# Gathering the dense products of a two-layer attention kernel into fewer key tiles

## The chip, the cores and the metric

The kernel runs on one core of one Trainium2 chip. The metric is the device time of one execution in microseconds, the median of several runs. TensorE is called PE below, its weight loads PEld, VectorE DVE, ScalarE ACT, GpSimd POOL and SyncE SP.

## The reference

Four sequences of 512 tokens with 256 channels pass through two attention layers with 16 heads of 16 channels.

```python
# layer 0
xn  = x * rsqrt(mean(x * x) + 1e-6) * rms_w
ss  = cond @ w_cond                         # scale, shift: 256 each
xm  = xn * (1 + scale) + shift
q, k, v = split(xm @ w_qkv)                 # q and k are rotated (rope)
x = softmax(q k^T / 4) v @ w_out + x
# layer 1
xn = layer_norm(x, norm_w, norm_b)
q, k, v = xn @ q_w + q_b, xn @ k_w + k_b, xn @ v_w + v_b      # and a mask
y  = softmax(q k^T + mask) v
e  = silu(cond) @ emb_w + emb_b             # scale, shift
h  = layer_norm(y, sb_norm_w, sb_norm_b) * (1 + scale) + shift
x  = x + silu(h) @ out_w + out_b
```

## The kernel before, in words

**Groups and key tiles.** The work is cut into 32 groups of four heads: groups 0 to 15 are layer 0, four for each batch, and 16 to 31 are layer 1. Step s of the main loop handles group s, in four key tiles k = 0 to 3 of 128 keys. A key tile (s, k) is the list `KEY_TILE`: four score products (L564) with four shift products that subtract the row maxima (L576), four row-score products of group s + 2 whose maxima DVE takes (L585, L961, and L958 in layer 1), and the product of the preceding key tile's probabilities with the values (L602). ACT takes the exponentials (L787). The first L602 of a tile's values is a good marker of time: `values(s, k)` stands near the end of tile (s, k + 1).

**One order for all engines.** `order()` writes out one list of operations. PE, ACT and DVE each walk through that list, so each meets its work in that order and waits there, in place, for what it needs. PE runs nothing out of order: if one operation in the list must wait, all behind it wait.

**Pieces.** Everything that isn't attention is cut into pieces, which the table `PIECES` puts into key tiles: `turn` (transposes of normalised tokens, L633), `qk` (one of four 128-channel chunks of queries and keys, L648), `v` (one of two halves of the values, L659), `y` (one of two halves of the output projection, L676), `modulate` and `embed` (the two products with the condition: step 0 at L687, step 1 at L695). The pieces of a tile stand behind its second row-score product and ahead of the other two.

**The row maxima's way back to PE.** The last row-score product of group n stands at the end of tile (n - 2, 3). DVE takes its maximum; then `negate(n)` on POOL (L1238, L1241, L1243) makes the shift; then `turn_shift(n)` on PE (L610), in tile (n - 1, 1) just ahead of the values, turns it. `turn_shift` waits for `negate`.

**POOL's program** is written out by hand and runs in order. For batch b of layer 1 it normalises the tokens (`normalise`), divides layer 0's outputs of the next batch by their sums (`divide`, without which `y` can't begin), splits query and key chunks into high and low parts (`split`, or `rope` for layer 0) and sends them to HBM through its own DMA queue (L1489), adds the values' bias (`add_bias`, L1299 and L1302, once for each half) and has the `negate` calls in between. SP loads the parts back (`operands`) and carries the shifts and outputs.

Of the kernel before, what the change touches and what calls it, by code (L numbers as in the profile page):

```python
# [12 lines left out]
P = 128  # L13
# [57 lines left out]
def v(layer, b):  # L71
    return ("v", layer, b, 0), ("v", layer, b, 1)
# [14 lines left out]
def one(pair):  # L87
# [34 lines left out]
for _b in range(B):  # L122
    STATISTICS[6 + NG * _b, 1] = ("p1", _b, 0)
    STATISTICS[6 + NG * _b, 2] = ("p1", _b, 1)
for _b in range(B - 1):
    STATISTICS[20 + NG * _b, 3] = ("f1", _b, None)

# [207 lines left out]
def build(nc, x, condT, mask, tables, vecs, w_cond, w_qkv, w_out, w_qkv1, v_b, emb_w, out_w, out_b, out):  # L335
# [4 lines left out]
    with ExitStack() as ctx:  # L340
# [39 lines left out]
        m.conditions = sb("conditions", [P, COND])  # L380
        m.chosen = sb("chosen", [P, B])
        m.e = sb("e", [P, KC, B])
        m.mod0_scale = sb("mod0_scale", [P, CT, B])
        m.mod0_shift = sb("mod0_shift", [P, CT, B])
        m.mod1 = sb("mod1", [P, 2, CT, B])
# [72 lines left out]
        q.es_step = sem("es_step")  # L458
        q.chosen_step = sem("chosen_step")
        q.acc_zero = sem("acc_zero")  # L460
# [87 lines left out]
def tensor(nc, pe, m, q):  # L548
# [131 lines left out]
    def conditioning(piece, vector):  # L680


        kind, step = piece
        if step == 0:
            bank = a_free(A[piece])
            for k in range(KC):
                last = nc.tensor.matmul(bank[W32 * k:W32 * (k + 1), :], vector[:, k, :], m.wc[:, k, :],  # L687
                                        start=True, stop=True, tile_position=(0, W32 * k), skip_group_check=True)
            last.then_inc(q.a_made, 1)
        else:  # L690
            bank = d_free(D[piece])
            pe.wait_ge(q.chosen_step, B)
# [84 lines left out]
def scalar(act, m, q):  # L777
# [27 lines left out]
    def tokens(piece):  # L805
        _, kind, b, h = piece
        use = USES.index((kind, b))
        if piece == ("turn", "p0", 0, 1):
            return
        if use >= 2 and kind != "f1":  # L810
            await_read(act, q, use - 2)
        to = m.xT[use % 2][:, h, :]
        if kind == "f1":
            act.wait_ge(q.d_done, D[piece] + 1)
            if b:
                act.wait_ge(q.silu_made, CT * (b - 1) + h + 1)
            act.activation(m.tanh[h], m.halved[h], ACT.Tanh).then_inc(q.tanh_made, 1)
            return
        bank = made(A[piece])
        if kind == "p0":  # L820
            if b:
                act.wait_ge(q.d_done, D["modulate", 1] + 1)
            act.wait_ge(q.mod_made, CT)
            act.activation(to, bank, ACT.Identity, bias=m.mod0_shift[:, h, b:b + 1], scale=m.mod0_scale[:, h, b:b + 1])\
# [79 lines left out]
    for op, *at in order():  # L904
# [6 lines left out]
        if op == "piece":  # L911
# [25 lines left out]
def vector(dve, m, q):  # L937
# [58 lines left out]

    def statistics(kind, b, src, t0, tiles):
        for t in range(t0, t0 + tiles):
            stat(dve.bn_stats(m.stats[:, TPB * b + t, :], src(t)))
# [16 lines left out]

    def take_statistics(kind, b, j):
        if kind == "p1":
            dve.wait_ge(q.d_done, D["y", 0, b, j] + 1)
            statistics(kind, b, lambda t: m.X[:, TPB * b + t, :], 2 * j, 2)  # L1020
        else:
            dve.wait_ge(q.d_done, D["output", NG * (B + b) + NG - 1] + 1)
            statistics(kind, b, lambda t: m.O[b % 2][:, t, :], 0, TPB)
        if j != 0:
            aggregate(kind, b)

    def opening():
# [50 lines left out]
    def rope_end(i):  # L1078
        dve.wait_ge(q.high_made, i + 1)
        dve.tensor_tensor(m.parts[:, 1, i, :], m.roped[0][i % 2][:, :], m.parts[:, 0, i, :], ALU.subtract)\  # L1080
           .then_inc(q.part_dve, 1)

    def modulate():
        bank = made(D["modulate", 1])[:, 0:KC * B].rearrange("p (k b) -> p k b", b=B)
        dve.wait_ge(q.vecs_in, 16)
        dve.tensor_copy(m.mod0_shift[:, :, :], bank[:, CT:2 * CT, :]).then_inc(q.mod_made, 1)
        dve.tensor_scalar(m.mod0_scale[:, 0, :], bank[:, 0, :], 1.0, m.vecs[:, RMS_W:RMS_W + 1], ALU.add, ALU.mult)\
           .then_inc(q.mod_made, 1)
        dve.tensor_scalar(m.mod0_scale[:, 1, :], bank[:, 1, :], 1.0, m.vecs[:, RMS_W + 1:RMS_W + 2], ALU.add, ALU.mult)\
           .then_inc(q.d_done, 1)  # L1090
# [4 lines left out]
        dve.tensor_scalar(m.xT[0][:, 1, :], half_turned, m.mod0_scale[:, 1, 0:1], m.mod0_shift[:, 1, 0:1],  # L1095
                          ALU.mult, ALU.add).then_inc(q.d_done, 1)
# [12 lines left out]
    def embed():  # L1109
        bank = made(D["embed", 1])[:, 0:KC * B].rearrange("p (k b) -> p k b", b=B)  # L1110
        dve.scalar_tensor_tensor(m.e[:, :, :], bank, 0.5,
                                 m.vecs[:, EMB_B:EMB_B + KC].unsqueeze(2).broadcast_to([P, KC, B]),
                                 ALU.mult, ALU.add).then_inc(q.d_done, 1)

# [90 lines left out]
def gpsimd(pool, m, q):  # L1205
# [57 lines left out]

    def rope(b, i, *shifts, send=True):


# [9 lines left out]
        pool.wait_ge(q.rope_pool, 4 * n + 2)  # L1276
        pool.tensor_tensor(x[:, :], x[:, :], z[:, :], ALU.add if two else ALU.subtract).then_inc(q.rope_pool, 1)
        pool.wait_ge(q.rope_pool, 4 * n + 3)
        await_parts(pool, q, b - 1, i)
# [3 lines left out]
        for n in shifts:  # L1283
            negate(n)
        if send:
            send_parts(b, i)

# [28 lines left out]
    for op, *at in order():  # L1316
        if op == "statistics" and at[2] != 0:
            moments_order.append(tuple(at[:2]))
    rstd_order = [u for u in NORMAL if u[0] != "p0"]
# [7 lines left out]
    pool.tensor_copy(m.ident16[:, :], m.ident[:, :]).then_inc(q.ident_made, 1)  # L1327
    pool.wait_ge(q.ident_made, 4)
    pool.tensor_copy(m.chosen[:, :], m.ident[:, 0:B]).then_inc(q.chosen_step, 1)
    for k in range(1, KC):  # L1330
        pool.wait_ge(q.chosen_step, k)
        pool.tensor_tensor(m.chosen[:, :], m.chosen[:, :], m.ident[:, W32 * k:W32 * k + B], ALU.add)\
            .then_inc(q.chosen_step, 1)
    for t in m.shift:
# [4 lines left out]
    for n in range(B):  # L1339
# [46 lines left out]
    negate(6)  # L1386
    divide(0, 0)
    divide(0, 1)
    rope(3, 0, 7)
    rope(3, 1, send=False)  # L1390

    def modulation():
        pool.wait_ge(q.d_done, D["embed", 1] + 1)
        for h in range(CT):
            for n, at in enumerate((SBN_W, SBN_B)):
# [25 lines left out]
    normalise(0)  # L1421
    send_parts(3, 1)
    divide(1, 0)
# [8 lines left out]
    split(B, 3)  # L1432
    add_bias(0, 0)
    for b in range(1, LAST):
# [4 lines left out]
        add_output_bias(b)  # L1439
        add_bias(b - 1, 1)  # L1440
        negate(NG * b + 9)
# [3 lines left out]
        split(B + b, 3)  # L1445
        add_bias(b, 0)
        divide(b + 1, 1)
# [3 lines left out]
    normalise(LAST)  # L1451
    add_output_bias(LAST)
    add_bias(LAST - 1, 1)
    negate(NG * LAST + 9)
# [216 lines left out]
```

## Time and profile before

| | |
|---|---|
| time of three runs | 492.68, 493.06, 494.52 us; median 493.06 us |
| the profiled execution | 493.28 us, span of its instructions 491.5 us |
| PE busy | 479.5 us, 98% |
| DVE, ACT, POOL busy | 79%, 70%, 64% |
| granted TensorE clock | 1.00 over the whole span |

The profiled execution is 0.22 us above the median of the runs. Busy time of PE is the union of overlapping products, and the end of each is modelled. So the start-to-start distances of PE's markers say more than its busy share.

### The profile page before, as it was taken

The page shows a single profiled execution, that of the slowest core. Times are in us where ns is not written, and L with a number is a line of the kernel's source. Part 1 is how long each engine was busy: PE and PEld are TensorE (multiplying, and loading weights), DVE is VectorE, ACT ScalarE, POOL GpSimd, SP SyncE. Part 2 cuts the span into 40 slices and gives each one's busy share as a digit, 9 for nine tenths or more (in the row PEclk, how much of TensorE's full clock was granted, in tenths as well). Part 3 has the DMA queues.
Part 4 walks back from the last instruction along what each step waited for, and adds up shares of the span by engine and source line. Part 5 has one row for each costly group of instructions (what it writes and reads, how often), then busy time and mean ns, then how long its engine had stood idle before and what let it go on. Part 6 is the DMA issues. An engine that isn't in the chain of part 4 may idle for free.

```text
span 491.5 us, 9721 instructions
## 1 busy us (share of the span) xinstructions
PE 479.5 (98%) x3205; PEld 178.4 (36%) x3205; DVE 386.1 (79%) x990; ACT 342.7 (70%) x676; POOL 314.2 (64%) x447
## 2 busy tenths in 40 slices
PE   7999899999999999999999999999999999999996
PEld 3563322323333334333343234333333323333234
DVE  3767896998886688856887688967899999999224
ACT  1662467898767786867767776776787778777853
POOL 6569976888798898699737692739991055005501
PEclk9999999999999999999999999999999999999999
DMA  7775157444423365225412361104411121111011
GB/s 244 197 206 194 45 135 264 112 115 149 112 66 115 111 183 149 68 68 140 123 54 67 107 187 44 46 24 126 114 45 44 45 88 45 44 45 45 2 43 43
DMA packets 41577, 49.79 MB, mean 101 GB/s; under 512 B 12388, under 2 KB 34036, under 8 KB 41272
## 3 DMA queue, kind: packets, MB, share of 16 engines
q1 hardware_dynamic: 33336, 31.84, 22.6%
q0 software_dynamic: 7904, 16.03, 10.9%
q10 hardware_dynamic: 288, 1.31, 0.8%
q8 instruction: 25, 0.41, 0.4%
q14 instruction: 24, 0.20, 0.1%
HBM read 27.62 MB, written 19.01 MB: 95 GB/s over the span
## 4 chain that ended last, share of the span: by engine, by line
PE 79%; DVE 14%; issue 3%; POOL 2%; ACT 1%; DVEq 0%; POOLq 0%; ACTq 0%
PE bank L602 20%; PE bank L648 12%; PE bank L576 11%; PE bank L585 11%; PE bank L564 9%; DVE masked L958 8%; PE bank L659 6%; PE bank L676 5%; DVE row_max L961 2%; PE bank L633 2%; ACT probs L787 1%; PE bank L617 1%; PE bank L610 1%; PE bank L734 1%; POOL shift L1335 1%
## 5 line engine op out<-in xcount | busy, mean ns | idle before, releaser
L787 ACT ACTIVATE probs<-bank 128x512 f32<-128x512 f32 x512 | 270.2, 599 | 71.3 <-PE bank L576 70.6
L961 DVE TENSOR_REDUCE row_max<-bank 128x1 f32<-128x512 f32 x256 | 159.9, 681 | 38.1 <-PE bank L585 37.9
L585 PE MATMUL bank<-k_s,q_s 64*128 64x512 f16 x512 | 179.9, 382 | 2.1 <-DVE row_max L961 1.2
L958 DVE CUSTOM_DVE_ANT_0 masked<-bank,mask_bias 128x512 bf16<-128x512 f32 x256 | 162.1, 687 | 20.3 <-PE bank L585 19.6
L564 PE MATMUL bank<-q_s,k_s 64*128 64x512 f16 x512 | 151.3, 380 | 0.3
L576 PE MATMUL bank<-shift,kx 64*128 64x512 f16 x512 | 148.7, 376 | 0.0
L602 PE MATMUL bank<-probs,v_aug 128*17 128x512 f32 x1024 | 135.4, 598 | 0.7 <-ACT probs L787 0.7
L585 PEld LDWEIGHTS bank<-k_s,q_s 64*128 64x128 f16 x512 | 46.2, 93 | 154.6 <-DVE row_max L961 67.4
L1238 POOL TENSOR_SCALAR scaled<-row_max 128x16 f32<-128x16 f32 x30 | 7.7, 256 | 86.3 <-DVE row_max L958 49.0
L648 PE MATMUL bank<-xT,wqkv 128*128 128x512 f32 x128 | 59.6, 605 | 1.0 <-DVE xT L1095 0.6
L576 PEld LDWEIGHTS bank<-shift,kx 64*128 64x128 f16 x512 | 46.9, 95 | 33.4
L1489 POOL DMA_DIRECT2D q_parts<-parts x60 | 34.8, 585 | 5.7 <-ACT parts L895 4.8
L1489 POOL DMA_DIRECT2D k_parts<-parts x62 | 35.1, 572 | 3.4 <-ACT parts L895 3.3
L564 PEld LDWEIGHTS bank<-q_s,k_s 64*128 64x128 f16 x512 | 32.8, 94 | 11.7 <-ACT probs L787 7.4
L648 PEld LDWEIGHTS bank<-xT,wqkv 128*128 128x128 f32 x128 | 22.9, 189 | 30.0 <-issue 26.9
L659 PE MATMUL bank<-wqkv,xT 128*128 128x256 f32 x128 | 31.3, 389 | 0.0
L602 PEld LDWEIGHTS bank<-probs,v_aug 128*17 128x17 f32 x1024 | 17.8, 95 | 30.6 <-ACT probs L787 14.5
L676 PE MATMUL bank<-wo,xT 128*128 128x256 f32 x112 | 27.9, 392 | 0.0
L659 PEld LDWEIGHTS bank<-wqkv,xT 128*128 128x128 f32 x128 | 23.2, 190 | 8.6 <-issue 5.4
L1015 DVE TENSOR_TENSOR X<-bank,X 128x512 f32<-128x512 f32 x14 | 9.6, 687 | 18.7 <-PE bank L676 18.7
L849 ACT ACTIVATE plain<-bank 128x512 f32<-128x512 f32 x16 | 9.5, 595 | 19.7 <-PE bank L648 19.7
L676 PEld LDWEIGHTS bank<-wo,xT 128*128 128x128 f32 x112 | 20.1, 189 | 8.1 <-DVE row_max L958 3.0
(122 smaller groups left out, 480.6 us busy)
## 6 DMA issues: line engine op xcount, KB each, us to landing
q_s<-q_parts SPq DMA_DIRECT2D x32, 256.0 KB, 3.3
k_s<-k_parts SPq DMA_DIRECT2D x32, 256.0 KB, 4.4
k_parts<-parts POOLq DMA_DIRECT2D x62, 128.0 KB, 3.2
q_parts<-parts POOLq DMA_DIRECT2D x60, 128.0 KB, 3.0
X<-in_x SPq DMA_DIRECT2D x4, 512.0 KB, 7.1
O<-oT SPq DMA_DIRECT2D x64, 32.0 KB, 2.0
roped<-inverses SPq DMA_DIRECT2D x16, 128.0 KB
y<-X SPq DMA_DIRECT2D x7, 256.0 KB, 2.2
```

The costliest lines, as they stand in the source:

```text
L564: nc.tensor.matmul(bank, m.k_s[slot][rows, i, keys], m.q_s[slot][rows, i, :], start=True, stop=False)
L576: nc.tensor.matmul(a_bank(m, A["score", s, k, h]), keys, m.shift[s % SHIFTS][rows, i, :], start=False, stop=True).then_inc(q.a_made, 1)
L585: nc.tensor.matmul(bank, m.q_s[slot][rows, i, queries], m.k_s[slot][rows, i, :], start=True, stop=True).then_inc(q.d_made, 1)
L602: last = nc.tensor.matmul(m.ACC[W32 * h:W32 * h + W, :], m.v_aug[pu % VALUES][:, k, G * g + h, :], m.probs[k][:, h, :], start=(k == 0), st ...
L633: last = nc.tensor.transpose(bank[:, t * P:(t + 1) * P], src[:, t, h * P:(h + 1) * P], m.ident[:, :])
L648: last = nc.tensor.matmul(bank, m.wqkv[layer][:, k, i * P:(i + 1) * P], m.xT[use % 2][:, k, :], start=(k == 0), stop=(k == CT - 1))
L659: last = nc.tensor.matmul(bank[:, t * C:(t + 1) * C], m.xT[use % 2][:, k, at], m.wqkv[layer][:, k, 2 * C:3 * C], start=(k == 0), stop=(k = ...
L676: last = nc.tensor.matmul(bank[:, t * C:(t + 1) * C], m.xT[use % 2][:, k, at], m.wo[layer][:, k, :], start=(k == 0), stop=(k == CT - 1))
L787: act.activation(m.probs[k][:, h, :], bank, ACT.Exp, scale=1.0 if s >= B * NG else float(DH) ** -0.5)\
L958: dve.tensor_tensor_reduce(m.masked[D["max", n, k, h] % ND][:, :], bank, m.mask_bias[:, b, :], 1.0, LOWEST, ALU.add, ALU.max, to)\
L961: dve.tensor_reduce(to, bank, AX.X, ALU.max).then_inc(q.d_done, 1)
L1489: engine.dma_start(to, m.parts[:, part, i, :]).then_inc(signal, 16)
```

## The change

The pieces are laid together. For every batch both halves of `y` of layer 0 stand in tile (6 + 4b, 1), where one stood in tile 0 and one in tile 1; both halves of the values stand in tile (6 + 4b, 2), where the first half stood earlier, in a tile of its own ((4, 2) for batch 3 of layer 0, (9 + 4b, 0) for layer 1); all four query and key chunks of a layer-1 batch stand in tile (7 + 4b, 3), where chunks 2 and 3 stood in tile (8 + 4b, 1). The last batch's values stand together in tile (20, 3). The statistics of a batch's four token tiles are all taken in tile (6 + 4b, 2).

The condition's product is turned by four transposes with the identity, where eight instructions multiplied it with a matrix `chosen` that POOL built; DVE adds the four partial rows with a reduction. One token tile of the opening's normalisation goes from DVE to ACT. Two small operations on `e` go from DVE to POOL.

On POOL, `rotate(3, 0)` stands between the two divisions of batch 0, the parts of `rope(3, 1)` are sent at once, and both halves of `add_bias(b - 1)` stand behind all splits of batch b, ahead of `divide(b + 1, 1)`. Before, one half of `add_bias(b - 1)` stood ahead of `negate(4b + 9)` and one half of `add_bias(b)` stood at the later place.

```diff
-    4: ((), (), v(0, 3)[:1], ()),
...
-    _other = v(0, 3)[1:] if _b == 0 else v(1, _b - 1)[1:]
-    PIECES[_s] = (*one(y(0, _b)), _other, ())
-    PIECES[_s + 1] = ((), (), turn("p1", _b), qk(1, _b, 0, 1))
-    PIECES[_s + 2] = ((), qk(1, _b, 2, 3), (), ())
-    PIECES[_s + 3] = (v(1, _b)[:1], (), (), ())
-PIECES[20] = ((), qk(1, LAST, 2, 3), (), v(1, LAST)[:1])
-PIECES[21] = (v(1, LAST)[1:], (), (), ())
+    PIECES[_s] = ((), y(0, _b), v(1, _b - 1) if _b else v(0, 3), ())
+    PIECES[_s + 1] = ((), (), turn("p1", _b), qk(1, _b, 0, 1, 2, 3))
+PIECES[20] = ((), (), (), v(1, LAST))
...
-    STATISTICS[6 + NG * _b, 1] = ("p1", _b, 0)
-    STATISTICS[6 + NG * _b, 2] = ("p1", _b, 1)
+    STATISTICS[6 + NG * _b, 2] = ("p1", _b)
...
-                last = nc.tensor.matmul(bank[:, c * B:(c + 1) * B], m.conditions[:, c * P:(c + 1) * P], m.chosen[:, :],
-                                        start=True, stop=True)
+                last = nc.tensor.transpose(bank[:, c * P:(c + 1) * P], m.conditions[:, c * P:(c + 1) * P], m.ident[:, :])
...
+            if piece == ("modulate", 0):
+                act.wait_ge(q.rstd0_made, 1)
+                act.activation(m.XN[0][:, TPB - 1, :], m.X[:, TPB - 1, :], ACT.Copy,
+                               scale=m.rstd["p0"][:, TPB - 1:TPB]).then_inc(q.xn0_made, 1)
...
-        for t in range(TPB):
+
+        for t in range(TPB - 1):
             normal_tile(dve, m, "p0", m.X[:, 0:TPB, :], m.XN[0], t, t).then_inc(q.xn0_made, 1)
...
+        dve.tensor_reduce(m.mod0[:, :, :], by_chunk(made(D["modulate", 1])), AX.X, ALU.add).then_inc(q.mod_made, 1)
...
     divide(0, 0)
+    rotate(3, 0)
     divide(0, 1)
-    rope(3, 0, 7)
-    rope(3, 1, send=False)
+    rotated_parts(3, 0, 7)
+    rope(3, 1)
...
     normalise(0)
-    send_parts(3, 1)
     divide(1, 0)
...
     split(B, 3)
-    add_bias(0, 0)
     for b in range(1, LAST):
         normalise(b)
         divide(b + 1, 0)
         if b == 1:
             add_output_bias(0)
         add_output_bias(b)
-        add_bias(b - 1, 1)
         negate(NG * b + 9)
         for i in range(3):
             split(B + b, i)
         negate(NG * b + 10)
         split(B + b, 3)
-        add_bias(b, 0)
+        add_bias(b - 1, 0)
+        add_bias(b - 1, 1)
         divide(b + 1, 1)
         negate(NG * b + 11)
         if b == 1:
             modulation()
     normalise(LAST)
     add_output_bias(LAST)
+    add_bias(LAST - 1, 0)
     add_bias(LAST - 1, 1)
     negate(NG * LAST + 9)
```

## Rows read from the trace of the kernel before

**Rows 1.** The page: span, and busy time of PE.

```profile
span 491.5 us, 9721 instructions
...
PE 479.5 (98%) x3205; PEld 178.4 (36%) x3205; DVE 386.1 (79%) x990; ACT 342.7 (70%) x676; POOL 314.2 (64%) x447
```

**Rows 2.** The chain that ended last: start, length, engine, output, line, instructions.

```profile
10.78 0.88 DVE XN L932 x3
11.80 1.08 PE bank L633 x8
...
25.30 6.87 PE bank L648 x16
...
94.80 0.99 PE bank L695 x8
...
128.30 0.98 PE bank L602 x8
130.04 1.92 PE bank L676 x8
...
154.73 3.63 PE bank L648 x8
```

**Rows 3.** Timeline of PE, values of tiles (6, 2) and (6, 3): start, length.

```profile
143.99 1.05 PE L602 MATMUL bank<-probs,v_aug 128*17 128x512 f32 x8
...
146.48 1.05 PE L602 MATMUL bank<-probs,v_aug 128*17 128x512 f32 x8
```

**Rows 4.** Timeline of PE, the values behind `turn_shift` of groups 8, 10, 14, 18, 22.

```profile
149.41 1.05 PE L602 MATMUL bank<-probs,v_aug 128*17 128x512 f32 x8
...
179.51 1.05 PE L602 MATMUL bank<-probs,v_aug 128*17 128x512 f32 x7
...
235.35 1.08 PE L602 MATMUL bank<-probs,v_aug 128*17 128x512 f32 x8
...
291.30 1.08 PE L602 MATMUL bank<-probs,v_aug 128*17 128x512 f32 x8
...
351.22 1.08 PE L602 MATMUL bank<-probs,v_aug 128*17 128x512 f32 x8
```

**Rows 5.** Timeline of POOL: `negate` 8, 9, 10, 13, 14, `add_bias`, `divide`, `negate` 17, 18, 21, 22.

```profile
148.30 0.27 POOL L1238 TENSOR_SCALAR scaled<-row_max 128x16 f32<-128x16 f32 x1
...
161.24 0.25 POOL L1238 TENSOR_SCALAR scaled<-row_max 128x16 f32<-128x16 f32 x1 [2.95 <-DVE row_max L961]
...
176.25 0.25 POOL L1238 TENSOR_SCALAR scaled<-row_max 128x16 f32<-128x16 f32 x1
...
217.07 0.25 POOL L1238 TENSOR_SCALAR scaled<-row_max 128x16 f32<-128x16 f32 x1 [0.50 <-DVE row_max L961]
...
230.67 0.25 POOL L1238 TENSOR_SCALAR scaled<-row_max 128x16 f32<-128x16 f32 x1 [0.20 <-DVE row_max L961]
...
235.70 0.93 POOL L1299 TENSOR_SCALAR v_bias<-vb_row,vecs 128x256 f32<-128x256 f32 x1
...
239.24 1.27 POOL L1312 TENSOR_TENSOR xT<-O,roped 128x512 f32<-128x512 f32 x1
...
272.99 0.25 POOL L1238 TENSOR_SCALAR scaled<-row_max 128x16 f32<-128x16 f32 x1 [3.31 <-DVE row_max L958]
...
287.32 0.25 POOL L1238 TENSOR_SCALAR scaled<-row_max 128x16 f32<-128x16 f32 x1
...
330.37 0.25 POOL L1238 TENSOR_SCALAR scaled<-row_max 128x16 f32<-128x16 f32 x1 [7.57 <-DVE row_max L958]
...
348.06 0.25 POOL L1238 TENSOR_SCALAR scaled<-row_max 128x16 f32<-128x16 f32 x1
```

**Rows 6.** Timeline of DVE: the statistics of a half batch.

```profile
195.97 0.74 DVE L999 BATCH_NORM_STATS2 stats<-X 128x6 f32<-128x256 f32 x2
```

**Rows 7.** Timeline of PE in the opening; in brackets the idle time before.

```profile
1.17 5.37 PE L702 MATMUL bank<-idle 128*128 128x512 f16 x17 [1.17 <-DVE idle L1028]
8.56 1.06 PE L687 MATMUL bank<-wc,condT 128*32 128x512 f32 x8 [2.01 <-DMA wc<-in_w_cond]
```

More of the change, by code:

```diff
@@ L458, in build @@
         q.es_step = sem("es_step")
-        q.chosen_step = sem("chosen_step")
+        q.embed_step = sem("embed_step")
         q.acc_zero = sem("acc_zero")
@@ L823, in tokens @@
             act.wait_ge(q.mod_made, CT)
-            act.activation(to, bank, ACT.Identity, bias=m.mod0_shift[:, h, b:b + 1], scale=m.mod0_scale[:, h, b:b + 1])\
+            act.activation(to, bank, ACT.Identity, bias=m.mod0[:, CT + h, b:b + 1], scale=m.mod0_scale[:, h, b:b + 1])\
                 .then_inc(q.a_done, 1)
@@ L995, in write_output, with statistics @@
            .then_inc(q.d_done, 1)
-    def statistics(kind, b, src, t0, tiles):
-        for t in range(t0, t0 + tiles):
+    def statistics(kind, b, src):
+        for t in range(TPB):
             stat(dve.bn_stats(m.stats[:, TPB * b + t, :], src(t)))
@@ L1015, in residual, with take_statistics @@
         dve.tensor_tensor(to, bank.rearrange("p (t c) -> p t c", c=C), to, ALU.add).then_inc(q.d_done, 1)
-    def take_statistics(kind, b, j):
+    def take_statistics(kind, b):
         if kind == "p1":
-            dve.wait_ge(q.d_done, D["y", 0, b, j] + 1)
-            statistics(kind, b, lambda t: m.X[:, TPB * b + t, :], 2 * j, 2)
+            dve.wait_ge(q.d_done, D["y", 0, b, 1] + 1)
+            statistics(kind, b, lambda t: m.X[:, TPB * b + t, :])
         else:
             dve.wait_ge(q.d_done, D["output", NG * (B + b) + NG - 1] + 1)
-            statistics(kind, b, lambda t: m.O[b % 2][:, t, :], 0, TPB)
-        if j != 0:
-            aggregate(kind, b)
+            statistics(kind, b, lambda t: m.O[b % 2][:, t, :])
+        aggregate(kind, b)
     def opening():
@@ L1081, in rope_end, with by_chunk @@
            .then_inc(q.part_dve, 1)
+    def by_chunk(bank):
+        return bank.rearrange("p (c k w) -> p c w k", k=KC, w=W32)[:, :, 0:B, :]
     def modulate():
[L1084 removed]
+        dve.tensor_reduce(m.mod0[:, :, :], by_chunk(made(D["modulate", 1])), AX.X, ALU.add).then_inc(q.mod_made, 1)
         dve.wait_ge(q.vecs_in, 16)
[L1086 to L1087 removed]
+        dve.wait_ge(q.mod_made, 1)
+        dve.tensor_scalar(m.mod0_scale[:, 0, :], m.mod0[:, 0, :], 1.0, m.vecs[:, RMS_W:RMS_W + 1], ALU.add, ALU.mult)\
            .then_inc(q.mod_made, 1)
[L1089 to L1090 removed]
+        dve.tensor_scalar(m.mod0_scale[:, 1, :], m.mod0[:, 1, :], 1.0, m.vecs[:, RMS_W + 1:RMS_W + 2],
+                          ALU.add, ALU.mult).then_inc(q.d_done, 1)
         half_turned = made(D["turn", "p0", 0, 1])
@@ L1109, in embed @@
     def embed():
[L1110 to L1113, printed above, removed]
+        dve.tensor_reduce(m.e[:, :, :], by_chunk(made(D["embed", 1])), AX.X, ALU.add).then_inc(q.d_done, 1)
     def last_batch():
@@ L1262, in split, with rotate @@
         send_parts(pu, i)
-    def rope(b, i, *shifts, send=True):
+    def rotate(b, i):
         side, two = divmod(i, 2)
@@ L1277, in rope, with rotated_parts @@
         pool.tensor_tensor(x[:, :], x[:, :], z[:, :], ALU.add if two else ALU.subtract).then_inc(q.rope_pool, 1)
+    def rotated_parts(b, i, *shifts):
+        n = 4 * (b - 1) + i
+        x = m.roped[0][0]
         pool.wait_ge(q.rope_pool, 4 * n + 3)
@@ L1284, in rope @@
             negate(n)
-        if send:
-            send_parts(b, i)
+        send_parts(b, i)
+    def rope(b, i, *shifts):
+        rotate(b, i)
+        rotated_parts(b, i, *shifts)
     def add_bias(b, j):
@@ L1316, in gpsimd @@
     for op, *at in order():
-        if op == "statistics" and at[2] != 0:
-            moments_order.append(tuple(at[:2]))
+        if op == "statistics":
+            moments_order.append(tuple(at))
     rstd_order = [u for u in NORMAL if u[0] != "p0"]
@@ L1327, in gpsimd @@
     pool.tensor_copy(m.ident16[:, :], m.ident[:, :]).then_inc(q.ident_made, 1)
[L1328 to L1333, printed above, removed]
     for t in m.shift:
@@ L1349, in gpsimd @@
             pool.wait_ge(q.xn0_made, TPB)
+            pool.wait_ge(q.d_done, D["modulate", 1] + 1)
             for a in range(2):
@@ L1387, in gpsimd @@
     divide(0, 0)
+    rotate(3, 0)
     divide(0, 1)
-    rope(3, 0, 7)
-    rope(3, 1, send=False)
+    rotated_parts(3, 0, 7)
+    rope(3, 1)
     def modulation():
         pool.wait_ge(q.d_done, D["embed", 1] + 1)
+        pool.tensor_scalar(m.e[:, :, :], m.e[:, :, :], 0.5, None, ALU.mult).then_inc(q.embed_step, 1)
+        pool.wait_ge(q.embed_step, 1)
+        pool.tensor_tensor(m.e[:, :, :], m.e[:, :, :],
+                           m.vecs[:, EMB_B:EMB_B + KC].unsqueeze(2).broadcast_to([P, KC, B]), ALU.add)\
+            .then_inc(q.embed_step, 1)
+        pool.wait_ge(q.embed_step, 2)
         for h in range(CT):
```

9 lines of the change are left out of this document (4 added, 5 removed).

## The prediction

> **What bounds the kernel now.** I read the page first. PE is busy for 98% of the span [rows 1], so one may think that only less PE work can help. Next I read the chain of waits. From step 6 to step 20 it is PE's own lines one after another, and the timeline of PE shows the same as a rhythm: two plain key tiles lie 146.48 - 143.99 = 2.49 us apart [rows 3], and a tile with pieces is longer by the pieces' own time. So PE sets the pace, and the other three engines follow with some slack. How much slack is what decides here. PE meets its waits in order, so a result that comes late stops everything behind it. The timeline of POOL shows where the slack is small. In the first row of [rows 5] `negate(8)` begins at 148.30, and the values that stand behind its turn begin at 149.41 [rows 4]: 1.11 us from the start of `negate` to that marker when PE is already there and waits. The marker before it is at 146.48 [rows 3], so that tile took 2.93 us against 2.49: PE lost some 0.45 us there, to POOL. Everywhere else PE comes later than POOL. I take 1.11 us as the price from `negate` to the marker, and ask for each later `negate` how long ahead of PE it was, and how much PE work the change removes between its two ends.
>
> **What the change saves on PE.** A block of eight fp32 instructions (one half of `y` or of the values) takes 1.92 us in the chain, a block of twice the work 3.63 us [rows 2]. Two blocks laid together therefore save 2 x 1.92 - 3.63 = 0.21 us, the cost of going from the half-height fp16 products to full fp32 ones and back. Sixteen instructions took 6.87 us in the opening, where other fp32 work follows [rows 2]; with one way back of some 0.2 us that is 7.05, and 2 x 3.63 - 7.05 = 0.21 us again. Blocks that vanish: four of `y`, four of `qk`, four of `v` in the tiles (6 + 4b, 2), one for the last batch: 13 x 0.21 = 2.7 us. The bounds are 13 x 0.15 and 13 x 0.3, 2 to 4 us.
>
> The embed step of 0.99 us becomes four transposes; eight take 1.08 us [rows 2], so 0.54, a saving of 0.45 us at most, 0.35 taken. In the opening the chain goes over DVE's normalisation, 0.88 us for three tiles [rows 2]; a fourth moved to ACT takes 0.29 us off it. ACT has just copied the condition and is idle. Since a later DMA wait may swallow some of this, I take 0.2 us, bounds 0 and 0.3. The turned condition of the opening is made while DVE still normalises, so its shorter form is hidden behind that. The extra reduction and its wait on DVE (three small operations before, three after) come to nothing within 0.1 us; the transposes of the tokens run meanwhile. The two operations on `e` fall on POOL behind `negate(15)`, where it next waits for statistics. If that cover were gone they would cost some 0.5 us.
>
> The statistics of the first two token tiles, 0.74 us [rows 6], move one tile down, into DVE's queue ahead of the maxima of tile (6 + 4b, 2). PE is then in the 3.63 us block of the values and DVE would be idle. Without this cover they would delay the maxima by 0.74 us for each batch, 3 us in all; I take nothing.
>
> Batch 0's `negate(8)` gets away from its wait: the `y` block is one tile later but the parts of `rope(3, 1)` are sent ahead of it, and `normalise(0)` begins when the statistics do, 4 to 5 us behind the `y` block's tile. By the same sum as above it ends about 1.5 us before PE comes. That gives back the 0.45 us. Savings together: 2.7 + 0.35 + 0.2 + 0.45 = 3.7 us.
>
> **What it costs: the `negate` behind the splits.** All four chunks now stand in tile (7 + 4b, 3), ahead of the last row scores of group 9 + 4b. POOL waits for that group's maxima in `negate(9 + 4b)` (the releaser in the brackets is DVE's row_max [rows 5]), then does a rope or three splits with their sends, then `negate(10 + 4b)`. That POOL work is as long as before. But between the same two ends PE had chunks 2 and 3, 3.63 us, and a first half of the values, 1.92 us, together 5.55 us, and both are gone from there: six plain tiles remain, 6 x 2.49 = 14.9 us. The slack before was:
>
> - Batch 0: `negate(10)` begins at 176.25, plus 1.11 is 177.36; the marker is at 179.51 [rows 4, 5]. Slack 2.15, so PE waits 5.55 - 2.15 = 3.4 us. From the other side: POOL's work from 161.24 to 176.25 is 15.0 us without a gap.
> - Batch 1: 230.67 + 1.11 against 235.35, slack 3.57, and POOL's own wait of 0.20 goes too. PE waits 5.55 - 3.77 = 1.8 us.
> - Batch 2: 287.32 + 1.11 against 291.30, slack 2.87: 2.7 us. The same POOL work took 14.33 us here and 13.60 for batch 1, 0.2 of it a wait; without that stretch it would be 1.8 us. I take 2.3.
> - Batch 3: from `negate(21)` to `negate(22)` lie four splits; 348.06 + 1.11 against 351.22, slack 2.05. Here 3.63 goes, and of the values 2 x 1.92 become 3.63, which still stand in this stretch. PE waits 3.63 + 0.21 - 2.05 = 1.8 us.
>
> Sum: 3.4 + 1.8 + 2.3 + 1.8 = 9.3 us.
>
> **What it costs: `add_bias` ahead of `divide`.** For batches 1 and 2 POOL then has `negate`, one split, now four token tiles of bias in place of two, and `divide(b + 1, 1)`, for which `y` waits. Two token tiles take 239.24 - 235.70 = 3.54 us [rows 5]. From the start of `negate(14)` to the end of the division: 235.70 - 230.67 = 5.03, plus 2 x 3.54, plus 1.27, together 13.4 us. PE, which has just been released, has 1.11 us to its marker, three plain tiles of 2.49, and 130.04 - 128.30 = 1.74 us [rows 2] from that marker to the `y` block: 10.3 us. So it waits 3.1 us more in batch 1. In batch 2, a layer-1 tile with a turned output lies between, some 0.6 us by the row of the transposes: 2.5 us more. Both waits stop PE with scores, maxima and exponentials queued behind them. Nothing makes up for it, since PE sets the pace after them too. For batch 0 the division stands right behind one split and is early. Sum: 5.6 us. The bounds of both sums: if POOL gained 1 us in each of the four stretches, 9.3 + 5.6 would be 10.9; if the stretch of batch 2 repeats and transfers stretch others alike, some 17.
>
> SP is passed too: `operands(12)` waits for the parts of `rope(3, 3)`, which POOL now sends later by the wait in `negate(9)`. Row scores of group 12 begin two steps on, and I count at least 3 us of slack, so nothing; if it is gone, the same 2 to 3 us of delay would show as a wait for `k_s`.
>
> **The sum.** 493.3 - 3.7 + 9.3 + 5.6 = 504.5 us for a profiled execution, 504.3 against the median.
>
> **The rivals.**
>
> *PE alone counts (faster).* If POOL is ahead of each `turn_shift` and each `y`, only the savings are left: 493.1 - 3.7 = 489.4 us. For it speaks that PE shows hardly a wait now. It needs POOL to save over 3.4 us of its 15 us between `negate(9)` and `negate(10)`, and nothing in the diff takes an operation out of there. It decides from that point: as long as the slack lost is above the slack of 2 to 3.8 us shown, PE stops. Chance 0.07.
>
> *The `negate` waits come, the `y` waits don't.* If `add_bias` runs in gaps, 489.4 + 9.3 = 498.7 us. Against it: POOL has no gap between `negate(14)` and the division. Chance 0.08.
>
> *The clock falls.* PE would stand still for 3.4, 3.1, 2.5 us at three places. The longest stop in the trace that didn't lower the clock is 2.01 us [rows 7]: the granted clock is 1.00 throughout. What a low clock costs shows in the opening: 17 idle products took 5.37 us where full speed (2.4 GHz, 0.213 us each, the step of 1.2 GHz being 0.43) takes 3.6, so 1.75 us. Three such places: 5 us more, 509.5. Chance 0.12. The Trainium skill, TensorE: Matmul & The Clock Gate, Part 1, says that a gate halves PE's clock after idling and opens it again after activity; by it this rival is what a stop of this kind does, and no row here has a stop so long.
>
> *Little change.* Savings and waits cancel if only one of the six waits comes and is small: within 0.5% (some 2.5 us, which is about what a measurement here can tell from no change). Chance 0.04.
>
> **How the numbers follow.** The forecast of 504.3 us has 0.69. The bounds of its terms, savings of 3 to 5 us and waits of 11 to 17, give 499 to 507. With the clock rival above it and the second rival below, the range 498.5 to 509 us leaves out the faster and the small cases and the tails. Faster 0.07, same 0.04, slower 0.89.
>
> **What would show it.** In the profile after, the tile behind `turn_shift(10)` has a gap on PE of about 3.4 us, with the releaser L1243 on POOL; so have groups 14, 18 and 22 with 1.8 to 2.7. The `y` products of tiles (14, 1) and (18, 1) wait for L1312. Tiles with two halves are 2.49 + 3.63 us apart and the tile with four chunks 9.5. POOL shows no idle time from `negate(13)` to `divide(2, 1)`. If these gaps are missing or POOL is idle there, the prediction is wrong. It is wrong too if the row scores or DVE are what PE waits for after the 7 us block, or if a granted clock below 1 shows behind a gap.

## The result and the profile after

The changed kernel takes 508.99 us (507.76 to 511.14, 4 runs) against 492.87 us (492.66 to 494.52, 4 runs): a ratio of 1.033, interval 1.029 to 1.036. The forecast was 504.3 us, with a range of 498.5 to 509.0. The profiled execution took 509.28 us, its span is 507.1 us, 15.6 us more than before [rows 1].

The page of the changed kernel, span and busy time:

```profile
span 507.1 us, 9703 instructions
...
PE 481.4 (95%) x3197; PEld 182.3 (36%) x3197; DVE 385.5 (76%) x989; ACT 343.0 (68%) x677; POOL 313.7 (62%) x445
```

PE has about as much work as before (479.5 us) and 15.6 us more span. The view of waits says for whom PE waited: line and releaser, us in total, times, longest.

```profile
PE bank L603 <- POOL neg_max L1240: 9.0, 4, 3.3
PE bank L669 <- POOL xT L1317: 4.6, 2, 3.4
PE bank L680 <- DMA wc<-in_w_cond: 1.3, 1, 1.3
...
PE bank L569 <- DMA shift<-shift_rows: 0.7, 1, 0.7
```

The timeline of PE has each of these waits; the number in brackets is the idle time ahead of the instruction.

```profile
128.16 0.39 PE L569 MATMUL bank<-shift,kx 64*128 64x512 f16 x2 [0.70 <-DMA shift<-shift_rows]
...
180.97 0.22 PE L603 MATMUL bank<-ident,neg_max 128*32 128x128 f16 x1 [3.31 <-POOL neg_max L1240]
...
238.04 0.22 PE L603 MATMUL bank<-ident,neg_max 128*32 128x128 f16 x1 [1.68 <-POOL neg_max L1240]
...
250.81 5.38 PE L669 MATMUL bank<-wo,xT 128*128 128x256 f32 x16 [3.40 <-POOL xT L1317]
...
301.16 0.22 PE L603 MATMUL bank<-ident,neg_max 128*32 128x128 f16 x1 [2.42 <-POOL neg_max L1240]
...
313.94 3.69 PE L669 MATMUL bank<-wo,xT 128*128 128x256 f32 x16 [1.23 <-POOL xT L1317]
...
366.78 0.22 PE L603 MATMUL bank<-ident,neg_max 128*32 128x128 f16 x1 [1.60 <-POOL neg_max L1240]
```

L603 is `turn_shift` of groups 10, 14, 18 and 22, L669 `y` of batches 2 and 3. The timeline of POOL answers to [rows 5]: `negate` 9 and 10, then 13 and 14, the first `add_bias`, and the division.

```profile
164.89 0.25 POOL L1235 TENSOR_SCALAR scaled<-row_max 128x16 f32<-128x16 f32 x1 [7.12 <-DVE row_max L957]
...
180.00 0.25 POOL L1235 TENSOR_SCALAR scaled<-row_max 128x16 f32<-128x16 f32 x1
...
223.58 0.25 POOL L1235 TENSOR_SCALAR scaled<-row_max 128x16 f32<-128x16 f32 x1 [8.37 <-DVE row_max L957]
...
237.07 0.25 POOL L1235 TENSOR_SCALAR scaled<-row_max 128x16 f32<-128x16 f32 x1
...
242.11 0.93 POOL L1304 TENSOR_SCALAR v_bias<-vb_row,vecs 128x256 f32<-128x256 f32 x1
...
249.41 1.26 POOL L1317 TENSOR_TENSOR xT<-O,roped 128x512 f32<-128x512 f32 x1
```

From `negate(9)` to `negate(10)` POOL takes 15.1 us, before 15.0; from 13 to 14 it takes 13.5, from 14 to the end of the division 13.6 where the prediction had 13.4. POOL's work is what it was, and from `negate(13)` to the end of the division it stands idle for 0.2 us only. What changed is that PE has less to do meanwhile. And POOL now stands idle for 7 to 8 us ahead of `negate(9)` and `negate(13)`, behind which its longest stretches begin.

One line above is odd. The `y` block of 16 instructions takes 5.38 us at 250.81 and 3.69 us at 313.94. The view by windows shows why; the columns are the stretch, its length, busy time and count for PE, PEld, DVE, ACT and POOL, the granted clock, the DMA share and GB/s.

```profile
246.00:252.00 6.00, 2.60 (x18) 1.23 (x11) 2.32 (x8) 2.32 (x5) 5.32 (x9) 0.94 0.38 112
252.00:258.00 6.00, 6.00 (x31) 3.60 (x31) 2.46 (x5) 1.22 (x3) 2.06 (x9) 0.78 0.00 0
...
300.00:305.00 5.00, 3.84 (x22) 1.37 (x23) 1.79 (x8) 1.35 (x3) 4.69 (x10) 0.74 0.74 225
305.00:312.00 7.00, 7.00 (x56) 1.84 (x54) 6.38 (x20) 5.10 (x10) 6.22 (x9) 0.94 0.33 99
```

The granted clock falls to its lower level, 1.2 GHz, for some 3 us behind two of the waits. It stays at 1.00 behind the other waits, behind the first one of 3.31 us too (windows 180 to 184 and 184 to 188). The four runs have mean clocks of 0.993, 0.989, 0.993 and 0.989: in each of them it fell somewhere.

**The balance,** by the distances of the values' markers against those of before: the four waits for `negate` cost 3.50, 1.87, 2.62 and 1.79 us, together 9.8; the two waits for the division 3.4 and 1.3, together 4.7; the low clock 1.75 us in the first `y` block and 1.54 us in tile (17, 2), which took 4.66 in place of 3.12 us; the late shift of group 6 in tile (6, 0) 1.48 us (0.70 of it is the wait for L569, the rest is spread over the tile). That is 19.2 us of loss for 15.6 us of span, so 3.6 us were saved. Added up from the tiles themselves, the savings are 3.7 us: 2.6 us for the thirteen blocks (0.20 each), 0.40 for the embed tile (3.07 in place of 3.47 us), 0.45 for tile (7, 1), and 0.25 in the opening.

### The profile page after: what moved, and what is told of

Same layout as the page of the kernel before. It is cut to its first block, busy times and chain, and to the rows that moved or that the text cites. A ratio compares the mean times of both kernels' runs of the same rounds, so it can differ in the third digit from the quotient of the medians.

```text
span 507.1 us, 9703 instructions
## 1 busy us (share of the span) xinstructions
PE 481.4 (95%) x3197; PEld 182.3 (36%) x3197; DVE 385.5 (76%) x989; ACT 343.0 (68%) x677; POOL 313.7 (62%) x445
## 4 chain that ended last, share of the span: by engine, by line
PE 49%; POOL 19%; DVE 16%; issue 6%; DMA 4%; ACT 1%; SPq 0%; DVEq 0%; POOLq 0%; ACTq 0%
PE bank L595 13%; DVE masked L954 9%; PE bank L569 7%; PE bank L641 6%; PE bank L578 6%; PE bank L557 6%; PE bank L669 5%; POOL k_parts L1495 3%; PE bank L652 3%; DMA k_parts<-parts 3%; POOL q_parts L1495 3%; POOL parts L1257 2%; DMA sums<-oT 2%; POOL roped L1273 2%; POOL roped L1270 1%
## 5 line engine op out<-in xcount | busy, mean ns | idle before, releaser
L569 PE MATMUL bank<-shift,kx 64*128 64x512 f16 x512 | 149.5, 378 | 0.7 <-DMA shift<-shift_rows 0.7
L569 PEld LDWEIGHTS bank<-shift,kx 64*128 64x128 f16 x512 | 46.9, 95 | 34.9 <-DMA shift<-shift_rows 1.2
L641 PE MATMUL bank<-xT,wqkv 128*128 128x512 f32 x128 | 58.5, 602 | 1.0 <-DVE xT L1095 0.6
L669 PE MATMUL bank<-wo,xT 128*128 128x256 f32 x112 | 28.5, 406 | 4.6 <-POOL xT L1317 4.6
L652 PE MATMUL bank<-wqkv,xT 128*128 128x256 f32 x128 | 30.0, 385 | 0.0
L595 PEld LDWEIGHTS bank<-probs,v_aug 128*17 128x17 f32 x1024 | 17.8, 95 | 29.3 <-ACT probs L779 16.1
L669 PEld LDWEIGHTS bank<-wo,xT 128*128 128x128 f32 x112 | 21.6, 200 | 11.8 <-issue 4.7
```

What stands on the lines that cost most here:

```text
L569: nc.tensor.matmul(a_bank(m, A["score", s, k, h]), keys, m.shift[s % SHIFTS][rows, i, :], start=False, stop=True).then_inc(q.a_made, 1)
L595: last = nc.tensor.matmul(m.ACC[W32 * h:W32 * h + W, :], m.v_aug[pu % VALUES][:, k, G * g + h, :], m.probs[k][:, h, :], start=(k == 0), st ...
L641: last = nc.tensor.matmul(bank, m.wqkv[layer][:, k, i * P:(i + 1) * P], m.xT[use % 2][:, k, :], start=(k == 0), stop=(k == CT - 1))
L652: last = nc.tensor.matmul(bank[:, t * C:(t + 1) * C], m.xT[use % 2][:, k, at], m.wqkv[layer][:, k, 2 * C:3 * C], start=(k == 0), stop=(k = ...
L669: last = nc.tensor.matmul(bank[:, t * C:(t + 1) * C], m.xT[use % 2][:, k, at], m.wo[layer][:, k, :], start=(k == 0), stop=(k == CT - 1))
```

## The experiments

Every kernel is timed together with the kernel before on the same chip; ratios are to it. Times in the expectations are medians, waits are those of profiles. The changed kernel is the base of each edit, unless the text says otherwise.

### Keeping PE busy in its waits

PE runs products of zeros, which belong to nothing, into the bank that is free anyway, ahead of each long wait and for less time than it.

```diff
+        keep_busy({10: 14, 14: 6, 18: 9, 22: 6}.get(n, 0), bank)      # in turn_shift
...
+                keep_busy({2: 14, 3: 5}.get(b, 0), bank)              # in tokens_out, layer 0
```

> The changed kernel with 54 idle products of PE in all, each batch of them just ahead of a wait of PE and shorter than that wait: 14, 6, 9 and 6 ahead of turn_shift 10, 14, 18 and 22, and 14 and 5 ahead of y of batches 2 and 3. They add nothing to the reference's result. Theory (the granted clock falls because PE stood still): the clock is 1.00 everywhere, the y block of batch 2 takes 3.6 us in place of 5.4, tile (17, 1) 3.1 in place of 4.7, the waits end at the same times, and the time falls by 3.3 us, to about 505.6 us. Rival (these stretches are slow for another reason, such as memory contention with POOL): no gain, 508.9 us or up to 1 us more.

506.52 us (506.38 to 506.81), ratio 1.027, interval 1.025 to 1.029. All four runs have a mean clock of 1.00, and they lie within 0.43 us, where those of the changed kernel lie within 3.4 us. The `y` block of batch 2 in PE's timeline, and the windows around it:

```profile
249.62 3.69 PE L673 MATMUL bank<-wo,xT 128*128 128x256 f32 x16 [0.43 <-POOL xT L1321]
```

```profile
240.00:250.00 10.00, 9.56 (x66) 3.30 (x63) 6.97 (x18) 6.15 (x13) 9.06 (x13) 1.00 0.54 144
250.00:260.00 10.00, 10.00 (x59) 6.33 (x57) 5.76 (x19) 3.63 (x9) 3.90 (x14) 1.00 0.06 13
```

The block takes 3.69 us again. (The slow tile that the expectation calls (17, 1) is (17, 2), by the distances of the markers; it takes 3.10 us here.) So the 5.38 us were the clock's, and the clock fell because PE stood still; POOL and the DMA queues had the same work in both. The gain in the medians is 2.5 us, less than the 3.3 us that one profile showed. Part of it came back as waits, since POOL's results are no earlier: tile (18, 1) took 9.12 us in place of 7.42, with five idle products and then 1.73 us of waiting for the division of batch 3, where PE waited 1.23 us in all. Part of the gain isn't the clock's either: between the two profiles 0.74 us lie in tile (6, 0) and 0.30 us in tile (2, 0), which vary from profile to profile.

### The bias ahead of `negate`

```diff
+        add_bias(b - 1, 0)
+        add_bias(b - 1, 1)
         negate(NG * b + 9)
...
-        add_bias(b - 1, 0)
-        add_bias(b - 1, 1)
         divide(b + 1, 1)
```

> The changed kernel with both halves of add_bias(b - 1) ahead of negate(4b + 9) in place of ahead of divide(b + 1, 1). POOL had 8.4 and 10.5 us without work there. Theory (POOL's program between negate(14) and the division is what y waits for): the two waits of PE for L1317, 3.40 and 1.23 us, vanish, the clock doesn't fall behind the first one (1.75 us back), and the four waits for negate stay as they are: 508.9 - 4.7 - 1.75, about 502.5 us. Rival (POOL is short of time as a whole, so its work only moves): negate(13) and negate(17) come late instead, and the time stays within 1.5 us of 508.9.

504.38 us (499.87 to 504.66), ratio 1.020, interval 1.016 to 1.025. The view of waits has no L1317 any more, and the four waits for `negate` stand at 9.2 us in all. So `add_bias` was what made `y` wait, and POOL had room for it elsewhere. The time is 1.9 us above the theory's, and its four runs say why: three with a mean clock of 0.99 took 504.3 to 504.7 us, the one with 1.00 took 499.87. In the profiled run the clock fell behind the first wait, of 3.35 us, which in the changed kernel's profile had left it alone (tile (9, 2) took 3.77 us for 2.49), and again in tile (17, 2), 4.66 us. The run at 1.00 is 4.4 to 4.8 us faster than the others, more than the 3.0 us that tiles (9, 2), (9, 3) and (17, 2) lost in the profile; where the rest went isn't known, since only one run has a trace.

### The chunks two and two

```diff
-    PIECES[_s + 1] = ((), (), turn("p1", _b), qk(1, _b, 0, 1, 2, 3))
-PIECES[20] = ((), (), (), v(1, LAST))
+    PIECES[_s + 1] = ((), (), turn("p1", _b), qk(1, _b, 0, 1))
+    PIECES[_s + 2] = ((), qk(1, _b, 2, 3), (), ())
+PIECES[20] = ((), qk(1, LAST, 2, 3), (), v(1, LAST))
```

> The changed kernel with chunks 2 and 3 back in tile (8 + 4b, 1); y and the values stay gathered. Theory (the gathered chunks take 3.63 us of PE work out of the stretch between two negates): the four waits for negate vanish, since only 1.9 us or less are missing there against a slack of 2.05 or more; y of batches 2 and 3 still waits, but only some 1.3 us each; the clock stays at 1.00. Four blocks more cost 4 x 0.21 us. 508.9 - 9.8 - 2.1 - 3.3 + 0.8, about 494.5 us. Rival (the gathered values cost most of it): above 500 us.

495.10 us (494.61 to 496.24), ratio 1.004, interval 1.003 to 1.006, clock 1.00 in all runs. One edit of a table brings back 13.9 of 16.1 us. The view of waits has no line for `negate`; the two waits for the division are left:

```profile
243.11 3.69 PE L670 MATMUL bank<-wo,xT 128*128 128x256 f32 x16 [1.59 <-POOL xT L1318]
...
301.17 3.69 PE L670 MATMUL bank<-wo,xT 128*128 128x256 f32 x16 [1.78 <-POOL xT L1318]
```

The gathered values, 1.9 us taken out of the same stretch, were within the slack of 2.05 us and more. Gathering the chunks wasn't.

### `negate` one split earlier

```diff
     rope(3, 3)
-    split(B, 0)
     negate(10)
+    split(B, 0)
...
-        for i in range(3):
+        for i in range(2):
             split(B + b, i)
         negate(NG * b + 10)
```

`negate(11)` and `negate(22)` move likewise, and part of the last batch's work behind `negate(22)` changes places.

> The changed kernel with each negate behind the splits moved ahead of one more split (negate(11) and negate(22) too), and nothing else: POOL does the same work up to each division. Theory (in batches 1 and 2 it is POOL's whole work up to divide that sets the end, not the place of negate): the waits for negate vanish, 9.8 us, but y of batches 2 and 3 now waits about 5 and 4 us in place of 3.4 and 1.2, so that only the parts of batch 0 and batch 3 and some of the clock come back: 508.9 - 3.5 - 1.8, about 503.5 us, with the clock falling behind one or both waits for y. Rival (the waits are separate from each other): all 9.8 us and one fall of the clock come back, about 497.5 us.

509.22 us (507.18 to 509.98), ratio 1.032, interval 1.029 to 1.034. The theory's two waits are there, and so are things that it didn't have:

```profile
183.96 0.39 PE L569 MATMUL bank<-shift,kx 64*128 64x512 f16 x2 [1.17 <-DMA shift<-shift_rows]
...
250.50 5.38 PE L669 MATMUL bank<-wo,xT 128*128 128x256 f32 x16 [3.96 <-POOL xT L1317]
...
313.67 6.43 PE L669 MATMUL bank<-wo,xT 128*128 128x256 f32 x16 [5.41 <-POOL xT L1317]
```

The waits for `negate` are gone and the waits for `y` have grown from 4.6 to 9.4 us: up to the division POOL has the same work, and PE is at the same place whichever of the two it waits for. That part stands. But the time is 5.7 us above what I expected. Both `y` blocks now run at the low clock (5.38 and 6.43 us). Shifts come late through SP's queue, and tiles (10, 0), (10, 1) and (14, 0) take 4.74, 7.74 and 4.46 us, 5.8 us more than in the changed kernel; two of the experiments below look into that.

### Half of the values back in tile (4, 2)

```diff
+    4: ((), (), v(0, 3)[:1], ()),
```

> The changed kernel with the first half of the values of batch 3 of layer 0 back in tile (4, 2). Theory (the wait for the shift of group 6 in tile (6, 0), 1.5 us, comes since PE is 1.9 us nearer to POOL's parts of batch 2, and SP's queue holds the shift behind the loads that wait for those parts): the wait vanishes, one more block costs 0.2 us, and the time is about 1.3 us lower, 507.6 us, which the times may hardly show but the profile does. Rival (rotate(3, 0) or the other order on POOL holds SP back): the wait stays and the time is 0.2 us higher.

509.00 us (507.32 to 510.54), ratio 1.032, interval 1.030 to 1.034. The wait for L569 is gone from the profile. SP's queue shows where it had come from. First the changed kernel, then this one: the last load of an inverse, the queries and keys of group 8, and the shift of group 6.

```profile
117.89 0.61 SPq L1574 DMA_DIRECT2D roped<-inverses  x1
123.84 0.36 SPq L1525 DMA_DIRECT2D q_s<-q_parts  x1
124.26 0.46 SPq L1525 DMA_DIRECT2D k_s<-k_parts  x1
124.82 0.61 SPq L1550 DMA_DIRECT2D sums<-oT  x1
125.53 1.38 SPq L1542 DMA_DIRECT2D shift<-shift_rows  x2
```

```profile
120.32 0.62 SPq L1575 DMA_DIRECT2D roped<-inverses  x1
121.12 0.36 SPq L1526 DMA_DIRECT2D q_s<-q_parts  x1
...
123.78 1.38 SPq L1543 DMA_DIRECT2D shift<-shift_rows  x2
```

In the changed kernel SP stands for 5.3 us between 118.5 and 123.84, ahead of the loads that wait for batch 2's parts, and sums and shift stand behind them in its queue. With PE 1.9 us later, SP doesn't wait. The time didn't fall for it: the wait for the division of batch 3 is 2.75 us in this profile in place of 1.23, and the `y` block behind it runs slow in place of tile (17, 2). Tile (9, 2), behind the first wait, runs slow too (3.98 us), which it didn't in the changed kernel's profile. With the clock falling at other places in each run, 1.3 us can't be seen in these times. The mechanism is shown, its price in the time isn't.

### What is left without the gathering

The pieces and `add_bias` are put back where they were. The transposed condition, the token tile on ACT, the statistics, `rotate(3, 0)` and `rope(3, 1)` stay changed.

> The changed kernel with the pieces spread over the key tiles as before, and add_bias at its places of before: what is left of the change is the condition turned by transposes, one token tile on ACT, the statistics taken together, and rotate(3, 0) and rope(3, 1) on POOL. Theory (the loss comes from the gathered pieces and add_bias alone): no wait of over 1 us on PE, clock 1.00, and 0.8 us less than before for opening and embed, 0.45 us more if negate(8) is in time: about 492.2 us. Rival (the statistics or the work moved to POOL cost something): at or above 493.1 us.

492.71 us (492.44 to 492.84, 10 runs), ratio 0.999, interval 0.998 to 1.000. PE has no wait of over 1 us behind the opening, and the clock is 1.00. So the loss comes from the gathering and `add_bias` alone. What the rest brings is 0.15 us in the medians, not 0.8 to 1.25, and the interval holds anything from no gain to 1.0 us. The profile shows where gains and losses lie: the tile with the embed step is 0.4 us shorter (3.08 for 3.47 us), tile (7, 1) 0.3, and the opening 0.25 from the first product with weights to the first transposes (2.99 us, where [rows 7] and [rows 2] give 11.80 - 8.56 = 3.24); tiles (11, 1) and (15, 1) are 0.26 us longer together. The first product with weights begins at 8.1 to 8.6 us from profile to profile, which is more than the opening saves.

### All chunks gathered, everything else mended

The diffs of three experiments together: `add_bias` early, the negates one split earlier, and half of the values back in tile (4, 2).

> The changed kernel with the three mends together: add_bias early as in the first experiment, the negates one split earlier, half of the values back in tile (4, 2). y, the other values and the chunks stay gathered. Theory (gathering saves 0.21 us a block, if POOL and SP are in time): no wait of PE above 0.7 us between steps 1 and 21, clock 1.00, and all savings kept, 0.8 + 0.45 + 12 x 0.21: 492.9 - 3.7, about 489.3 us. Rival (the stretches are too short for POOL in any order): waits stay, and the time is above 493 us.

494.87 us (493.87 to 496.88, 11 runs), ratio 1.004, interval 1.003 to 1.006: the theory's 489.3 us is missed by 5.6 us, and the rival's bound of 493 us is passed. Yet no wait for POOL is left, which the rival would have; these took their place:

```profile
183.34 0.39 PE L570 MATMUL bank<-shift,kx 64*128 64x512 f16 x2 [1.05 <-DMA shift<-shift_rows]
...
242.74 0.89 PE L579 MATMUL bank<-k_s,q_s 64*128 64x512 f16 x2 [0.91 <-DVE row_max L958]
```

Tiles (10, 0) and (10, 1) took 4.57 and 7.75 us, where 2.49 and 6.15 were due, and tile (14, 0) 4.54: 5.7 us together. The first two are SP again, with a low clock behind it in tile (10, 1): `operands(12)` waits for the parts of `rope(3, 3)`, with the sums of group 8 and the shift of group 10 behind it. The next experiment sends these parts earlier.

```diff
-    rope(3, 2, 9)
-    rope(3, 3)
+    rope(3, 2)
+    rotate(3, 3)
+    negate(9)
+    rotated_parts(3, 3)
```

> The kernel with all three mends (all chunks gathered, negates one split earlier) with rope(3, 2) and the rotation of rope(3, 3) ahead of negate(9), where POOL had 7.2 us without work, so that the parts of the last chunk are sent some 5 us earlier. Theory (the 3.7 us lost in tiles (10, 0) and (10, 1) come from SP, which holds the sums and the shift of group 10 behind the loads that wait for these parts): the wait for the shift of group 10 vanishes with its fall of the clock, 3 to 3.7 us in its profile, some 2.5 us in the median of its runs; 2 us in tile (14, 0) stay, where no such load waits. About 492.3 us. Rival (the DMA queues are full of the parts themselves, and the sums and shifts land late whatever the order): no gain, 494.9 us.

492.41 us (491.50 to 494.37, 11 runs), ratio 0.999, interval 0.998 to 1.000. The expectation was 492.3 us. Tiles (10, 0) and (10, 1) take 2.49 and 6.15 us. The theory of SP's queue holds there. Tile (14, 0) stays long, 5.09 us, with this row:

```profile
240.28 0.89 PE L579 MATMUL bank<-k_s,q_s 64*128 64x512 f16 x2 [1.31 <-DVE row_max L958]
```

Here no load waits for parts. In the kernel ahead of this one, SP issued the sums of group 12 at 235.76, DVE's reciprocal, which waits for them, ran at 241.79, and DVE's maxima stood behind it. All that time POOL's parts, SP's operands and the outputs were on their way, with a DMA share of 0.86. That the queues' load delays the sums is the reading; no run here took the load away, so it stays open.

### The versions that keep what pays

Chunks two and two with the bias early, by the two diffs above:

> The changed kernel with two mends: chunks 2 and 3 back in tile (8 + 4b, 1), and both halves of add_bias(b - 1) ahead of negate(4b + 9). y and the values stay gathered. Theory (gathering pays where POOL stays in time): the two waits of 1.6 and 1.8 us for the division, which the kernel with chunks two and two still had, vanish, no wait of PE above 0.7 us is left after step 1, and the nine blocks of y and values that are gone show as 9 x 0.21 us: 492.7 - 1.9, about 491.0 us, and below the kernel before. Rival (a wait of similar size takes the place of the ones removed): 493 us or more.

492.36 us (491.38 to 492.92, 11 runs), ratio 0.9987, interval 0.9978 to 0.9996. The waits for the division are gone, and one of 0.46 us for `negate(14)` has come. The theory's 491.0 us is missed by 1.4 us: the gain is 0.5 us, by its interval 0.2 to 1.1, where 1.9 was expected.

With half of the values back in tile (4, 2) as well:

> The kernel of the run before it with the first half of the values of batch 3 of layer 0 back in tile (4, 2) too. Theory: one block more, 0.2 us, against a wait for the shift of group 6 that was 0.15 to 0.7 us in the profiles without it: the same time within 0.4 us, with less spread. Rival (that wait is larger in undisturbed runs than the profiles show): 0.5 to 1.3 us faster.

492.04 us (491.44 to 492.38, 11 runs), ratio 0.9978, interval 0.9969 to 0.9986: 0.8 us below the kernel before, clear of noise, and within 0.4 us of the run ahead of it, as the theory had it. Its profile has one wait of 1.01 us for `negate(14)`, since two output biases and four token tiles of bias hold up `negate(13)`:

```profile
218.51 0.25 POOL L1237 TENSOR_SCALAR scaled<-row_max 128x16 f32<-128x16 f32 x1
...
232.03 0.25 POOL L1237 TENSOR_SCALAR scaled<-row_max 128x16 f32<-128x16 f32 x1
```

One output bias moved ahead of `normalise(1)`:

```diff
     split(B, 3)
+    add_output_bias(0)
     for b in range(1, LAST):
```

> The kernel with chunks two and two, bias early and half of the values back, with add_output_bias(0), 2.3 us of POOL, ahead of normalise(1), where POOL had some 3 us without work. In the kernel without this move negate(13) began at 218.51, 3.4 us later than its maxima allow, since the two output biases and four token tiles of bias stood ahead of it, and PE waited 1.01 us for negate(14). Theory: negate(13) and negate(14) come 2.3 us earlier, this wait vanishes, and the time is 1.0 us lower, 491.0 us against 492.0. Rival (normalise(1) is pushed back by it and PE waits for negate(12) or the transposes): no gain or a loss.

491.91 us (490.95 to 494.75, 12 runs), ratio 0.9980, interval 0.9964 to 0.9995: 0.8 us below the kernel before again, and no gain over the version ahead of it, where 1.0 us was expected. The wait for `negate(14)` is gone, and a wait for a shift stands in tile (14, 0), which takes 3.91 us for 2.49:

```profile
239.26 0.39 PE L571 MATMUL bank<-shift,kx 64*128 64x512 f16 x2 [0.95 <-DMA shift<-shift_rows]
```

Neither theory had that. In that stretch waits of 0.5 to 1.3 us for POOL, for SP's loads and for DVE took each other's place from version to version. Why the shift is late here wasn't tested.

## Why the prediction was right, and where it was off

The measured 508.99 us lies within the range, but only 0.01 us below its upper end, and that is luck: one run of the changed kernel was at 507.76, another at 511.14. The forecast itself was 4.7 us too low, and the rival with the falling clock, at 509.5 us, was nearer. By one of its own signs, "a granted clock below 1 shows behind a gap", the prediction was wrong in that part. What was right is the mechanism of the six waits and nearly all of their sizes.

**What sets the end.** Right. PE's work fell, as forecast, and the time rose, since PE came to POOL's results before POOL had them. All gaps that the prediction named are there, with the releasers that it named. The kernel with chunks two and two, which gives the stretches their PE work back, shows that this was the cause and not a cost of the gathered blocks themselves.

**Savings, 3.7 us forecast, 3.6 us in the balance.** The marker distances bear out the size of a block: tiles with two halves are 6.15 us and the tile with four chunks 9.55 us. `negate(8)` was in time: tile (7, 1) took 2.48 us. The opening's 0.2 us are in the profile (3.24 us became 2.98 from the first product with weights to the first transposes), and too small for the times.

**The waits for `negate`, 9.3 us forecast, 9.8 us measured**: 3.4, 1.8, 2.3, 1.8 against 3.50, 1.87, 2.62, 1.79. The way to them, slack of before less the PE work that goes, needed no knowledge of any unit's speed, and it came within 0.35 us four times. For batch 2 the plain subtraction gave 2.7 us, nearer to the 2.62 measured than the 2.3 that was taken.

**The waits for the division, 5.6 us forecast, 4.7 us measured.** Batch 2 is right (3.1 against 3.4). In batch 3 the forecast was 2.5 and the measured wait 1.3 us, because tile (17, 2) lost 1.5 us to the low clock, and POOL caught up by that much. With PE kept busy and the clock at 1.00, the two divisions cost 3.6 and 3.0 us by the markers, idle products included, so the term was some 0.5 us short for each. A late unit isn't late twice: what PE loses elsewhere in a stretch comes off its wait.

**The clock.** The step that failed is the choice of the likeliest case: "PE would stand still for 3.4, 3.1, 2.5 us at three places" was given a chance of 0.12, and it happened in each run. Its price was 5 us for three falls; two falls cost 3.3 us in the profile, and the kernel kept busy was 2.5 us faster. The 1.75 us for one fall were read from the opening, whose idle products were slow while the granted clock is shown as 1.00; the main loop, where it is shown falling, bears the size out with 1.75 and 1.54 us. The Trainium skill, TensorE: Matmul & The Clock Gate, Part 1, has the gate halve the clock after idling; this case agrees behind two of the six waits, with windows at 0.78 and 0.74.

**SP.** The statement "I count at least 3 us of slack, so nothing" looked at one wait only. The waiting instruction that mattered was `operands(8)`, one batch earlier, with the shift of group 6 behind it: 1.48 us in this profile, and 0.4 to 1.2 us in the five others that have both halves of the values in tile (6, 2). `operands(12)` itself had its slack only as long as PE waited for `negate(10)`; as soon as that wait was mended, SP's came up at the same tile.

With the clock's 3.3 and SP's 1.5 us, less the 0.9 us of the division and plus the 0.5 of `negate`, the forecast's 504.5 becomes 508.9 us. The 0.4 us that are left to the profiled 509.28 lie outside the span (509.28 - 507.1 against 493.28 - 491.5).

## What to carry to other kernels

When work is moved or merged on the unit that sets the pace, take for each result that it waits for the slack that the old profile shows, and subtract the work that has gone from between the result's start and its use; here each gathered batch took up to 5.5 us of cover away for some 0.6 us saved. Look at where a slower unit stands idle: POOL had 8 us free just ahead of the stretch in which it was late, and moving its work there paid, while moving a single result forward only moved the wait. Count a long stop of PE as dearer than its length: here some of the stops of 2.4 us and more had a low clock behind them, at 1.3 to 1.75 us a fall, and 2.7 us behind the longest.

## What the runs showed that was not expected

The clock doesn't follow the length of one stop. It stayed at 2.4 GHz behind a stop of 3.31 us in one profile, and fell behind a stop of 3.31 us at the same place in the kernel with half of the values back, and behind one of 2.42 us. In the kernel with all mends it fell in six of eleven runs; its profile, one of these six, has no stop of PE above 1.1 us from step 1 to step 21, and the stretch from 184 us has it low:

```profile
180.00:184.00 4.00, 2.82 (x22) 0.62 (x16) 2.01 (x5) 2.16 (x5) 3.98 (x6) 1.00 0.78 235
184.00:187.00 3.00, 2.87 (x15) 0.43 (x14) 2.70 (x5) 1.94 (x4) 2.17 (x6) 0.73 0.47 124
187.00:190.00 3.00, 3.00 (x16) 1.68 (x13) 1.39 (x2) 1.68 (x3) 3.00 (x6) 0.70 0.24 48
```

Most falls showed as some 3 us at half speed. In the kernel with `negate` one split earlier, where PE stood still for 5.41 us, the low stretch was longer and began during the stop:

```profile
308.00:314.00 6.00, 0.59 (x5) 0.36 (x2) 1.17 (x4) 1.17 (x3) 5.38 (x8) 0.87 0.08 28
314.00:320.00 6.00, 6.00 (x16) 4.56 (x15) 0.69 (x1) 0.00 (x0) 0.35 (x2) 0.56 0.00 0
```

A low clock also spreads the times, but it isn't alone in that: the runs of the changed kernel lie within 3.4 us and those of the kernel kept busy within 0.4, while eleven runs with chunks two and two and bias early, all at 1.00, lie within 1.5 us. The kernel before, too, has runs with a mean clock of 0.997 to 0.999 among its slowest (494.7 to 495.0 us), beside others of 494.5 us at 1.00.
